# Four-layer gated mix on Trainium2: the second attention's mask as one float32r product in place of two float16 products

## The chip, the cores and the metric

The kernel runs on one core of one Trainium2 chip. The metric is the time of one execution in device microseconds (us), read as the median of several runs. Instruction durations come from one profiled execution.

## What is computed

Four layers follow one another on x, 8 sequences of 128 tokens by 128 features. Each layer adds a gated attention-like part and then a gated feed-forward part. The change touches the attention of the second of the three softmax attentions (layer index 2), which has 16 heads of depth 8, a key mask and a matrix of group probabilities:

```python
logits = jnp.einsum('bhqd,bhkd->bhqk', q, k) / jnp.sqrt(jnp.asarray(dh, q.dtype))
neg = (1.0 - mask.astype(q.dtype)) * -1000000000.0
logits = logits + neg[:, None, :, :]
attn = jax.nn.softmax(logits, axis=-1)
attn = attn * group_prob[:, None, :, :]
out = jnp.einsum('bhqk,bhkd->bhqd', attn, v)
```

So -1e9 is added to every masked score of all 16 heads, in every sequence.

## The kernel before

The program is written engine by engine: PE (matrix products), DVE, ACT, POOL (elementwise) and SP (transfers) each run a fixed order of instructions, and counters (semaphores) tie them. Nothing is reordered at run time, so an instruction that waits holds up all that stand behind it on its engine.

Attention a = 1 (the one above) goes over 8 blocks b, one for each sequence. Heads go in four sets j = 0..3 of four heads; a set fills one PSUM bank of 128 x 512. For each block there are these steps:

- **Row scores**, `att_rows` (L1204): for two sets at a time (p = 0, then p = 1), 8 small products (L1214) give the scores with queries on the partitions; then, for each of the two sets, the mask is added by products of a diagonal matrix with the mask NMA, broadcast over the four heads (all products made through the helper `products` show as L194). I call the two halves R0 and R1.
- **Maxima**: DVE reduces each set (L1235). After the fourth, five small DVE instructions of 128 x 16, here called the split (`att_max_split`: L1245, L1247, L1249, L1251, L1253), write the maximum as three float16 parts. PE turns them (`att_max_pe`, L1266), and DVE adds them to the queries (L1275).
- **Column scores**, `att_cols` (L1278), halves C0 and C1: 8 small products (L1288) give scores minus maximum with keys on the partitions, and the mask NMB is added in the same way, to banks 2 and 3.
- ACT takes the exponential of each set (L1306), **POOL multiplies it by the group probabilities** (`att_group`, L1310), and PE sums (L1323) and applies the values (L1329) in `att_pv`.
- DVE normalises (L1337, L1341), ACT and DVE split the result in high and low parts (L1348, L1356), PE applies the output weights, DVE adds to X (L1374) and starts the next layer's norm: statistics (L338, L344), POOL makes the factor (L348, L350), DVE applies it (L354), PE turns it (L405).

PE's order within block b is: C0(b); R1(b+1); `att_pv` of block b-1 for sets 2 and 3; C1(b); L1266 for b+1; output product of b-2; R0(b+2); `att_pv` of block b for sets 0 and 1; from b = 3 on the turn L405 of block b-3; then C0(b+1). C0(b+1) needs the exponentials of block b and the queries of b+1; R1(b+1) needs the first two maxima of b+1; L1266 needs the whole split; from b = 3 on L405 needs the addition to X of block b-2.

DVE's order within block b is: maxima 0 and 1 of b+1; L1356 and L413 of earlier blocks; maxima 2 and 3 of b+1; split of b+1; normalise b-1; L1275 of b+1; L354 of b-3; L1374, L338, L344 of b-2.

The mask constant is made from two float16 diagonals, DGH (-61024 on the diagonal) and DGL (-11.15625), each times 16384 (NMA, NMB) where the key is masked. They are written once by DVE in `later_dve` (L312), in front of the first softmax attention.

Of the kernel before, what the change touches and what calls it, by code (L numbers as in the profile page):

```python
# [8 lines left out]
NB, S, D = 8, 128, 128  # L9
# [19 lines left out]

B_ROW = ((0, 1), (2, 3))  # L30

MASK_UNIT = 16384.0
MASK_HI, MASK_LO = -61024.0, -11.15625
ROUND = 1.5 * 2.0 ** 23
MAX_UNITS = (16384.0, 16.0, 1.0)

# [1 line left out]
def gated_mix_program(nc, t, out):  # L38
    fp32, fp16, bf16 = mybir.dt.float32, mybir.dt.float16, mybir.dt.bfloat16
    i32, u32 = mybir.dt.int32, mybir.dt.uint32  # L40
    ALU, ACT, AX = mybir.AluOpType, mybir.ActivationFunctionType, mybir.AxisListType.X

    ctx = ExitStack()
    with ctx:
        def sb(name, shape, dt=fp32):
            return ctx.enter_context(nc.sbuf_tensor(name, shape, dt))
# [3 lines left out]
        def sem(name):  # L50
            if name not in sems:
                sems[name] = ctx.enter_context(nc.semaphore(name))
            return sems[name]

        def over(ap, n):

            p, m = ap.shape
            return ap.unsqueeze(1).to_broadcast([p, n, m])
# [17 lines left out]
        EYE, EYEH = sb("EYE", [128, 128]), sb("EYEH", [128, 128], fp16)  # L76
# [12 lines left out]
        B1 = sb("B1", [128, CH0])  # L89
        B2F, B2H, B2L = sb("B2F", [E0, D]), sb("B2H", [E0, D], fp16), sb("B2L", [E0, D], fp16)  # L90
        GPT = sb("GPT", [128, NB, S])
        NMA, NMB = sb("NMA", [128, NB, S], fp16), sb("NMB", [128, NB, S], fp16)
        DGH, DGL = sb("DGH", [128, 128], fp16), sb("DGL", [128, 128], fp16)
        IOTA = sb("IOTA", [128, 8])
        CW = sb("CW", [128, NB, 128], fp16)
        CT = sb("CT", [128, TOK], fp16)
# [31 lines left out]
        def bank(i, n=1):  # L128
            return PS[:, 512 * i:512 * (i + n)]
# [61 lines left out]
        def products(pe, dst, pairs, start=True, stop=True):  # L191

            for i, (l, r) in enumerate(pairs):
                last = pe.matmul(dst, l, r, start=start and i == 0, stop=stop and i == len(pairs) - 1)  # L194
            return last
# [116 lines left out]
        def later_dve(dve):  # L312

            dve.wait_ge(sem("ld_brow"), 16)
            dve.tensor_copy(BH[:], BF[:]).then_inc(sem("b_split"), 1)
            dve.wait_ge(sem("b_split"), 1)
            dve.tensor_tensor(BL[:], BF[:], BH[:], ALU.subtract).then_inc(sem("b_split"), 1)
            dve.wait_ge(sem("ld_bqk"), 16)
            dve.wait_ge(sem("ld_lom"), 16)
            for a in range(2):  # L320
                dve.tensor_scalar(BQK[:, a, 0, :], BQK[:, a, 0, :], DH ** -0.5, None, ALU.mult).then_inc(sem("scaled"), 1)
            dve.wait_ge(sem("scaled"), 2)
            for i in range(2):
                dve.tensor_scalar(LOB[:, :, i, :], BQK[:, :, i, :], LOM[:, i:i + 1], None, ALU.mult).then_inc(sem("lob"), 1)
            dve.tensor_scalar(DGH[:], EYE[:], MASK_HI, None, ALU.mult).then_inc(sem("eyes"), 1)
            dve.tensor_scalar(DGL[:], EYE[:], MASK_LO, None, ALU.mult).then_inc(sem("eyes"), 1)
            dve.wait_ge(sem("ld_masks"), 16)
            for i, m in enumerate((NMA, NMB)):

                dve.tensor_scalar(m[:].rearrange("p b s -> p (b s)"), MI[:, i, :], -MASK_UNIT, MASK_UNIT,  # L330
                                  ALU.mult, ALU.add).then_inc(sem("eyes"), 1)
            dve.wait_ge(sem("ld_fb1"), 16)
            dve.tensor_scalar(FB1G[:], FB1[:], G[:, 5:6], None, ALU.mult).then_inc(sem("eyes"), 1)
# [870 lines left out]
        def att_rows(pe, a, b, p):  # L1204

            n = NB * a + b
            if p == 0 and b in (0, 4):
                pe.wait_ge(sem("p_lo"), PROJ * a + (14 if b == 0 else 18))
            if 4 * n + 2 * p:
                pe.wait_ge(sem("a_max"), 4 * n + 2 * p)  # L1210
            for g in range(4):
                for j in (2 * p, 2 * p + 1):
                    r = slice(32 * j, 32 * j + 3 * DH)
                    last = pe.matmul(bank(j % 2)[:, 128 * g:128 * g + 128], QU[r, g, b, :], KU[r, g, b, :],  # L1214
                                     start=g == 0, stop=a == 0 and g == 3)
                    if a == 0 and g == 3:
                        last.then_inc(sem("a_rows"), 1)
            for j in (2 * p, 2 * p + 1):
                if a == 1:
                    products(pe, bank(j % 2), [(d[:], over(NMA[:, b, :], 4)) for d in (DGH, DGL)], start=False)\  # L1220
                        .then_inc(sem("a_rows"), 1)
                if a == 2:
                    products(pe, bank(j % 2), [(FLIP[:], biased(TBH[:, 0], j))], start=False).then_inc(sem("a_rows"), 1)

        def biased(table, j):

            return table.rearrange("p (g j s) -> p g j s", g=4, j=4)[:, :, j, :]
# [50 lines left out]
        def att_cols(pe, a, b, u, p):  # L1278

            n = NB * a + b  # L1280
            if p == 0:
                pe.wait_ge(sem("a_qx"), n + 1)
            if 4 * n + 2 * p:
                pe.wait_ge(sem("a_exp"), 4 * n + 2 * p)
            for g in range(4):
                for j in (2 * p, 2 * p + 1):
                    r = slice(32 * j, 32 * j + 32)
                    last = pe.matmul(bank(2 + j % 2)[:, 128 * g:128 * g + 128], KU[r, g, b, :], QX[r, u, g, :],  # L1288
                                     start=g == 0, stop=a == 0 and g == 3)
                    if a == 0 and g == 3:  # L1290
                        last.then_inc(sem("a_cols"), 1)
            for j in (2 * p, 2 * p + 1):
                if a == 1:
                    products(pe, bank(2 + j % 2), [(d[:], over(NMB[:, b, :], 4)) for d in (DGH, DGL)], start=False)\
                        .then_inc(sem("a_cols"), 1)
                if a == 2:
                    products(pe, bank(2 + j % 2), [(FLIP[:], biased(tb[:, 1], j)) for tb in (TBH, TBL)], start=False)\
                        .then_inc(sem("a_cols"), 1)
# [81 lines left out]
        def att_pe(pe, a):  # L1380
            k, j = NEXT[a]
            if a == 2:
                pe.wait_ge(sem("t5_split"), 12)
                pe.wait_ge(sem("ld_flip"), 16)
            att_rows(pe, a, 0, 0)
            att_rows(pe, a, 0, 1)
            att_max_pe(pe, a, 0, 0)
            att_rows(pe, a, 1, 0)
            pe.wait_ge(sem("p_lo"), PROJ * (a + 1))
            for b in range(NB):  # L1390
                u = b % 2
                att_cols(pe, a, b, u, 0)
                if b + 1 < NB:
                    att_rows(pe, a, b + 1, 1)
                if b >= 1:
                    att_pv(pe, a, b - 1, 1 - u, 2)
                    att_pv(pe, a, b - 1, 1 - u, 3)
                att_cols(pe, a, b, u, 1)
                if b + 1 < NB:
                    att_max_pe(pe, a, b + 1, 1 - u)  # L1400
                if b >= 2:
                    att_out(pe, a, b - 2, u)
                if b + 2 < NB:
                    att_rows(pe, a, b + 2, 0)
                att_pv(pe, a, b, u, 0)
                att_pv(pe, a, b, u, 1)
                if j and b >= 3:
                    turn_one_pe(pe, a, j, k, b - 3)
# [260 lines left out]
        def _(dve):  # L1669
# [10 lines left out]
            route_dve(dve, 0)  # L1680
            moe_dve(dve, 0)
            later_dve(dve)
            norm_dve(dve, 2)
            proj_dve(dve, 0, "vk")
# [161 lines left out]
```

## Time and profile before

| | us |
|---|---|
| median of 3 runs | 740.63 |
| lowest, highest | 739.57, 746.64 |
| the profiled execution's own time | 742.89 |
| its span, first to last instruction | 741.1 |
| second softmax attention, first row scores to last turn (L405) | 273.45 to 359.5 |

The page gives busy shares of the span: PE 84%, DVE 78%, ACT 48%, POOL 43%. The span is divided into 40 slices of 18.5 us; the attention in question fills slices 15 to 19. "Granted clock" is 1.00 at TensorE's 2.4 GHz level and 0.50 at its 1.2 GHz level.

How to read it: in a timeline, the time between the starts of two products is what the first one occupies of PE. Its printed duration is longer, since products are pipelined (0.38 us for a product whose successor starts 0.22 us later). A bracket such as [0.40 <-ACT ...] is the idle time of that engine ahead of the row, and what ended it.

### The profile page before, as it was taken

To read this page: it belongs to the slowest core of one execution; us is meant where nothing else is said; L and a number is where in the kernel's file an instruction comes from. 1 tells how busy PE (TensorE), PEld (TensorE's weight loads), DVE (VectorE), ACT (ScalarE), POOL (GpSimd) and SP (SyncE) were. 2 spreads that over 40 slices of the span, in tenths; PEclk is the share of its full clock that TensorE was granted. 3 is DMA by queue.
4 is the path that set the end of the run, shared out by engine and by line. 5 is a ranking of instruction groups with operands and counts; after the bars stand their busy time and mean duration, and the time that the engine had idled before them with its cause. 6 is when DMAs were issued, how large, how long until landed. Compare 5 with 4: busy or idle time off the path is not lost.

```text
span 741.1 us, 16834 instructions
## 1 busy us (share of the span) xinstructions
PE 620.3 (84%) x5152; PEld 301.1 (41%) x5152; DVE 577.3 (78%) x1174; ACT 358.4 (48%) x665; POOL 315.7 (43%) x578
## 2 busy tenths in 40 slices
PE   3774999978676577998289999999999879994996
PEld 2432433433355233555134444444444424552442
DVE  6684877777797685787769999999999785675796
ACT  4645889854453161233045455545545472341543
POOL 2486677631047202767325455444444100225241
PEclk9986999986799597999589999999999897996899
DMA  8000111105000000000011112112112000000120
GB/s 280 3 1 18 44 47 46 47 16 139 1 3 3 0 1 1 3 2 2 12 34 53 50 52 57 53 51 57 53 50 58 19 1 2 2 3 12 37 52 29
DMA packets 42346, 25.78 MB, mean 35 GB/s; under 512 B 13308, under 2 KB 41224, under 8 KB 42168
## 3 DMA queue, kind: packets, MB, share of 16 engines
q1 hardware_dynamic: 41864, 24.38, 11.6%
q8 instruction: 32, 0.52, 0.3%
q10 hardware_dynamic: 432, 0.73, 0.3%
q14 instruction: 18, 0.15, 0.1%
HBM read 24.54 MB, written 0.56 MB: 34 GB/s over the span
## 4 chain that ended last, share of the span: by engine, by line
PE 61%; DVE 22%; POOL 7%; ACT 4%; issue 4%; DMA 0%; ACTq 0%; DVEq 0%; POOLq 0%
PE PS L194 50%; DVE SHARED L1201 4%; DVE MB L1235 3%; PE PS L1214 2%; PE PS L1323 2%; DVE MF L1235 2%; PE PS L1329 1%; DVE REC L1337 1%; ACT SHARED L939 1%; PE PS L1288 1%; POOL RSTD L350 1%; DVE XN L354 1%; DVE STAT L338 1%; POOL RSTD L376 1%; PE PS L1266 1%
## 5 line engine op out<-in xcount | busy, mean ns | idle before, releaser
L950 ACT ACTIVATE SHARED<-SHARED 128x512 f16<-128x512 f32 x180 | 113.4, 630 | 120.9 <-DVE SHARED L962 114.4
L968 DVE TENSOR_TENSOR SHARED<-SHARED 128x512 f16<-128x512 f32 x180 | 141.5, 793 | 28.1 <-ACT SHARED L950 27.5
L194 PE MATMUL PS<-XH,UH 128*128 128x512 f16 x296 | 114.3, 386 | 2.4 <-ACT CT L769 2.2
L194 PE MATMUL PS<-XL,UH 128*128 128x512 f16 x296 | 114.2, 386 | 0.0
L194 PE MATMUL PS<-XH,UL 128*128 128x512 f16 x296 | 114.2, 386 | 0.0
L194 PE MATMUL PS<-SHARED,DNH 128*128 128x512 f16 x360 | 107.1, 379 | 6.4 <-DVE SHARED L968 6.2
L1306 ACT ACTIVATE SHARED<-PS 128x512 f32<-128x512 f32 x96 | 52.4, 595 | 99.5 <-PE PS L194 75.2
L959 DVE TENSOR_TENSOR SHARED<-SHARED,PS 128x512 f32<-128x512 f32 x116 | 78.6, 678 | 11.4 <-PE PS L194 11.4
L881 POOL CAST DNH<-DF 128x128 f16<-128x128 f32 x90 | 30.4, 338 | 132.0 <-PE PS L194 132.0
L962 DVE TENSOR_TENSOR SHARED<-SHARED,PS 128x512 f32<-128x512 f32 x116 | 79.7, 687 | 4.0
L871 POOL TENSOR_TENSOR UL<-UF,UH 128x256 f16<-128x256 f32 (+1 forms) x90 | 71.6, 796 | 7.2
L194 PE MATMUL PS<-SHARED,DNL 128*128 128x512 f16 x180 | 68.2, 379 | 0.0
L934 ACT ACTIVATE SHARED<-PS 128x512 f32<-128x512 f32 x116 | 62.3, 584 | 4.7 <-PE PS L194 4.6
L1310 POOL TENSOR_TENSOR SHARED<-SHARED,GPT 128x512 f32<-128x512 f32 x32 | 40.0, 1270 | 42.8 <-ACT SHARED L1306 42.8
L869 POOL CAST UH<-UF 128x256 f16<-128x256 f32 (+1 forms) x90 | 42.0, 467 | 33.7 <-PE PS L194 30.3
L1235 DVE TENSOR_REDUCE MB<-PS 128x4 f16<-128x512 f32 x64 | 41.2, 688 | 19.0 <-PE PS L194 13.9
L194 PEld LDWEIGHTS PS<-SHARED,DNH 128*128 128x128 f16 x360 | 33.3, 97 | 53.1 <-issue 21.3
L939 ACT ACTIVATE SHARED<-PS,B 128x512 f32<-128x512 f32 x64 | 43.4, 678 | 10.9 <-PE PS L194 8.4
L194 PEld LDWEIGHTS PS<-XH,UH 128*128 128x128 f16 x296 | 29.2, 99 | 45.8 <-issue 11.5
L883 POOL TENSOR_TENSOR DNL<-DF,DNH 128x128 f16<-128x128 f32 x90 | 41.5, 461 | 7.2
L194 PE MATMUL PS<-CT,SEL 128*128 128x512 f16 x116 | 44.5, 383 | 0.0
L194 PEld LDWEIGHTS PS<-XH,UL 128*128 128x128 f16 x296 | 29.4, 99 | 36.2 <-issue 2.2
(272 smaller groups left out, 1108.1 us busy)
## 6 DMA issues: line engine op xcount, KB each, us to landing
UF<-in_up SPq DMA_DIRECT2D x58, 128.0 KB, 2.0
DF<-in_down SPq DMA_DIRECT2D x90, 64.0 KB, 1.8
UF<-in_up SPq DMA_DIRECT2D x32, 64.0 KB, 1.8
SHARED<-t_values_dram SPq DMA_DIRECT2D x2, 1024.0 KB, 11.2
SEL<-in_sel SPq DMA_DIRECT2D x58, 32.0 KB, 1.8
SHARED<-in_masks SPq DMA_DIRECT2D x1, 1024.0 KB, 6.7
WF<-in_wsmall SPq DMA_DIRECT2D x1, 808.0 KB, 6.7
X<-in_x SPq DMA_DIRECT2D x1, 512.0 KB, 3.5
```

The lines of the kernel that those rows point to most:

```text
L194: last = pe.matmul(dst, l, r, start=start and i == 0, stop=stop and i == len(pairs) - 1)
L869: pool.tensor_copy(UH[:, u, 0:n], UF[:, u, 0:n]).then_inc(sem("e_up_ready"), 1)
L871: pool.tensor_tensor(UL[:, u, 0:n], UF[:, u, 0:n], UH[:, u, 0:n], ALU.subtract)\
L883: pool.tensor_tensor(DNL[:, u, :], DF[:, u, :], DNH[:, u, :], ALU.subtract)\
L934: act.activation(SG[:, hf, :], bank(hf), ACT.Silu).then_inc(sem("e_act"), 1)
L939: act.activation(RH[u][:, hf, :], bank(hf), ACT.Relu, bias=B1[:, bass.ds(c, 1)]).then_inc(sem("e_act"), 1)
L950: act.activation(HHI[:, u, hf, :], (HF if M["gated"] else RH[u])[:, hf, :], ACT.Copy).then_inc(sem("e_high"), 1)
L959: dve.tensor_tensor(TG[:, hf, :], SG[:, hf, :], bank(2 + hf), ALU.mult).then_inc(sem("e_gated"), 1)
L962: dve.tensor_tensor(HF[:, hf, :], TG[:, hf, :], bank(4 + hf), ALU.mult).then_inc(sem("e_hidden"), 1)
L968: dve.tensor_tensor(HLO[:, u, hf, :], src[:, hf, :], HHI[:, u, hf, :], ALU.subtract).then_inc(sem("e_low"), 1)
L1235: dve.tensor_reduce(dst, src, AX, ALU.max, negate=True).then_inc(sem("a_max"), 1)
L1306: act.activation(PF[:, j, :], bank(2 + j % 2), ACT.Exp).then_inc(sem("a_exp"), 1)
```

## The change

The two float16 diagonals become one float32r diagonal, and the masks become float32r. 10000 = 625 x 16 and -100000 = -3125 x 32 multiply to -1e9 with 10 and 12 significant bits. Each mask addition is then one product in place of two: per block 8 products where there were 16.

```diff
-MASK_UNIT = 16384.0
-MASK_HI, MASK_LO = -61024.0, -11.15625
+MASK_UNIT = 625.0 * 16.0
+MASK_DIAG = -3125.0 * 32.0
@@ tiles
-        NMA, NMB = sb("NMA", [128, NB, S], fp16), sb("NMB", [128, NB, S], fp16)
-        DGH, DGL = sb("DGH", [128, 128], fp16), sb("DGL", [128, 128], fp16)
+        NMA, NMB = sb("NMA", [128, NB, S], f32r), sb("NMB", [128, NB, S], f32r)
+        DGH = sb("DGH", [128, 128], f32r)
@@ later_dve
-            dve.tensor_scalar(DGH[:], EYE[:], MASK_HI, None, ALU.mult).then_inc(sem("eyes"), 1)
-            dve.tensor_scalar(DGL[:], EYE[:], MASK_LO, None, ALU.mult).then_inc(sem("eyes"), 1)
+            dve.tensor_scalar(DGH[:], EYE[:], MASK_DIAG, None, ALU.mult).then_inc(sem("eyes"), 1)
@@ att_rows
-                    products(pe, bank(j % 2), [(d[:], over(NMA[:, b, :], 4)) for d in (DGH, DGL)], start=False)\
+                    products(pe, bank(j % 2), [(DGH[:], over(NMA[:, b, :], 4))], start=False)\
@@ att_cols
-                    products(pe, bank(2 + j % 2), [(d[:], over(NMB[:, b, :], 4)) for d in (DGH, DGL)], start=False)\
+                    products(pe, bank(2 + j % 2), [(DGH[:], over(NMB[:, b, :], 4))], start=False)\
```

## Rows read from the trace of the kernel before

**Rows 1.** Chain that ended last, in block 2: start, us, work.
```profile
304.36 0.55 PE PS L194 x2
...
306.25 0.62 DVE MB L1245
```

**Rows 2.** Timeline of PE, block 2: start, us, instruction.
```profile
302.66 0.40 PE L1288 MATMUL PS<-QX,SHARED 32*128 32x128 f16 x8
302.99 0.39 PE L194 MATMUL PS<-NMB,DGH 128*128 128x512 f16 x1
303.22 0.38 PE L194 MATMUL PS<-NMB,DGL 128*128 128x512 f16 x1
...
306.27 0.40 PE L1288 MATMUL PS<-QX,SHARED 32*128 32x128 f16 x8
...
307.82 0.40 PE L1266 MATMUL PS<-EYEH,MB 128*128 128x128 f16 x4 [0.18 <-DVE MB L1253]
...
310.73 0.40 PE L1288 MATMUL PS<-QX,SHARED 32*128 32x128 f16 x8
```

**Rows 3.** Timelines of ACT and POOL, block 2.
```profile
303.63 1.09 ACT L1306 ACTIVATE SHARED<-PS 128x512 f32<-128x512 f32 x2 [2.16 <-PE PS L194]
...
304.31 2.49 POOL L1310 TENSOR_TENSOR SHARED<-SHARED,GPT 128x512 f32<-128x512 f32 x2 [1.68 <-ACT SHARED L1306]
307.92 2.51 POOL L1310 TENSOR_TENSOR SHARED<-SHARED,GPT 128x512 f32<-128x512 f32 x2 [1.11 <-ACT SHARED L1306]
```

**Rows 4.** Timeline of DVE, block 2: parts of the split.
```profile
306.25 0.60 DVE L1245 TENSOR_SCALAR MB<-MF 128x16 f16<-128x16 f32 x1
...
307.35 0.18 DVE L1251 SCALAR_TENSOR_TENSOR MF<-MB,MF 128x16 f32<-128x16 f16 x1
307.56 0.20 DVE L1253 CAST MB<-MF 128x16 f16<-128x16 f32 x1
```

**Rows 5.** Timelines of POOL, DVE and PE around the split of block 1.
```profile
288.12 2.48 POOL L1310 TENSOR_TENSOR SHARED<-SHARED,GPT 128x512 f32<-128x512 f32 x2 [0.40 <-ACT SHARED L1306]
...
288.26 1.15 DVE L1251 SCALAR_TENSOR_TENSOR MF<-MB,MF 128x16 f32<-128x16 f16 x1
289.45 1.21 DVE L1253 CAST MB<-MF 128x16 f16<-128x16 f32 x1
...
290.72 0.40 PE L1266 MATMUL PS<-EYEH,MB 128*128 128x128 f16 x4 [2.88 <-DVE MB L1253]
...
294.61 0.60 PE L1288 MATMUL PS<-QX,SHARED 32*128 32x128 f16 x8
```

**Rows 6.** Timelines of PE and DVE in the later blocks.
```profile
327.54 0.30 PE L405 MATMUL PS<-EYE,XN 128*128 128x128 f32 x1 [0.19 <-DVE X L1374]
327.78 0.40 PE L1288 MATMUL PS<-QX,SHARED 32*128 32x128 f16 x8
...
334.29 1.42 DVE L354 TENSOR_SCALAR XN<-X,MV,RSTD 128x128 f32<-128x128 f32 x1
...
344.92 0.40 PE L1288 MATMUL PS<-QX,SHARED 32*128 32x128 f16 x8
```

**Rows 7.** Windows: us, busy (count) of PE, PEld, DVE, ACT, POOL, granted clock.
```profile
182.70:186.00 3.30, 3.30 (x8) 1.19 (x9) 0.75 (x1) 1.30 (x2) 0.00 (x0) 0.50 0.00 0
292.00:295.00 3.00, 3.00 (x42) 1.73 (x40) 1.38 (x2) 0.00 (x0) 0.00 (x0) 0.50 0.00 0
596.30:600.00 3.70, 3.63 (x20) 1.74 (x20) 3.70 (x6) 2.88 (x5) 0.00 (x0) 1.00 0.00 0
612.20:616.00 3.80, 2.84 (x24) 1.14 (x24) 1.72 (x3) 0.00 (x0) 0.00 (x0) 0.57 0.00 0
```

**Rows 8.** Lines L1523 and L330 (ns min/median/max), and a timeline row of L384.
```profile
L1523 PE MATMUL PS<-OH,RB x2: 1031/1044/1056, 52.7 to 53.6; 32*16 32x512 f32 x2
...
179.57 1.04 PE L384 MATMUL PS<-EYE,XN 128*128 128x128 f32 x8
...
L330 DVE TENSOR_SCALAR NMA<-SHARED x1: 684/684/684, 167.6 to 167.6; 128x1024 f16<-128x1024 int32 x1
```

More of the change, by code:

```diff
@@ L40, in gated_mix_program @@
     i32, u32 = mybir.dt.int32, mybir.dt.uint32
+    f32r = mybir.dt.float32r
     ALU, ACT, AX = mybir.AluOpType, mybir.ActivationFunctionType, mybir.AxisListType.X
```

## The prediction

> **What bounds the kernel now.** I read the page first (PE 84% busy, DVE 78%), then the chain of waits in the second softmax attention, then timelines of each engine for one block, since only there one sees who is late. In block 2 the chain runs through PE's mask products into DVE's maxima and the split [rows 1]: PE looks like the bound, 8.07 us from one C0 to the next (302.66 to 310.73) [rows 2], of which 16 mask products at some 0.22 us (302.99 to 303.22) are 3.5 us. But look further. POOL works in pairs of multiplies of 2.49 us, and the second pair starts 1.12 us after the first has ended (304.31 + 2.49 = 306.80; 307.92) [rows 3]. L1245 of the split, 0.20 us when free, starts at 306.25 and takes until 306.85, just after POOL's pair ends; the rest of the split then fits in the gap, its last instruction starting 0.36 us before POOL's second pair [rows 3, 4]. And around the split of block 1, where POOL's pair came 0.14 us ahead of L1251, L1251 took 1.15 us (until 289.41, POOL's first multiply ending near 289.36) and L1253 1.21 us (until 290.66, POOL's second ending at 290.60), against 0.18 and 0.20 [rows 4, 5]. So each of these DVE instructions waits for the end of the POOL multiply that is running. L354, 0.34 us when free, takes 1.42 us in the later blocks for the same reason [rows 6]. The kernel runs well as long as the split slips through POOL's gap.
>
> **The mask products, size.** A float16 product of 512 columns occupies 0.215 to 0.22 us. No row shows float32r. Bounds: a float32 product of 512 columns is two instructions 0.9 us apart at the low clock, so 0.9 us in all at the high one [rows 8]; that is the upper end. The middle: 8 float32 transposes of 128 columns take 1.04 us, 0.11 us each from start to start, so a single pass over 512 columns of float32 could be 0.43 us [rows 8]. The lower end is float16's 0.215 us. 
>
> **What that does in block 2 if each product is 0.215 us.** Four products go between C0 and C1: 4 x 0.2175 = 0.87 us. C0 to C1 is now 306.27 - 302.66 = 3.61 us, then 2.74 us. POOL's first pair starts 1.65 us after C0 now; one product fewer ahead of the first exponential makes it 1.43 us. It ends at C0 + 3.92. The second pair can start at 2.74 + 1.43 = C0 + 4.17: a gap of 0.25 us in place of 1.12 us. The maxima come 0.65 us earlier (three products), but that is worth nothing: L1245 waits for the end of the pair, and after it L1251 starts 0.55 us and L1253 0.76 us past the pair's end (307.35 and 307.56 against 306.80) [rows 4]. Now both find POOL busy, as in block 1. L1253 ends with POOL's second pair, at 4.17 + 2.49 + 0.05 = C0 + 6.71, and L1266 starts at C0 + 6.76 instead of 5.16 (307.82 - 302.66). Behind L1266 on PE stand the output product, R0 and `att_pv`, then the next C0: 2.91 us now, 2.48 us with two products fewer. A block takes 6.76 + 2.48 = 9.24 us, 1.17 us more than 8.07.
>
> **Later blocks.** They take 8.57 us (two from 327.78 to 344.92). Add the turn of 0.24 us (327.54 to 327.78) to the sum above [rows 6]: 9.48 us. The wait of PE for L1374 goes, since L354 now starts after POOL's pair. The last of the intervals has no R0 and is led by DVE: some 9.1 us. From C0 of block 1 to C0 of block 7 it is now 344.92 - 294.61 = 50.31 us [rows 5, 6]; then 2 x 9.24 + 3 x 9.48 + 9.1 = 56.0 us: **+5.7 us**.
>
> **Ends.** Blocks 0 and 1 already have the hold and a low clock; their mask products cost about 0.43 us each in the low stretch, and four of them go ahead of the second pair: -1.7 us, of which I keep -1.5 us (bounds -3 and 0). After the last C0 POOL's four multiplies run without a gap and set the end; only one product goes ahead of them: -0.2 us.
>
> **Clock.** In a block of 9.24 us, C1's last result is there 2.74 + 0.33 + 0.22 + 0.38 = 3.7 us after C0, and L1266 starts at 6.76: PE stands idle for 3.1 us. The kernel has six idle stretches of PE of 2.1 to 2.9 us that begin at the high clock, and after each of them the granted clock falls to the low level (0.50 to 0.58) for 3 us or more; after one of 1.9 us it doesn't (596.30 to 600.00 at 1.00) [rows 7] (the group has the stretch behind the first and the last of the six, and the one behind block 1's idle 2.88 us). In block 1 the stretch from L1266 to C0 took 294.61 - 290.72 = 3.89 us against 2.91, and the 8 products behind it 0.60 against 0.40 [rows 2, 5]: at least 1.2 us. Three us at half speed are 1.5 us lost if PE leads all the while. I take 1.4 us for each of six blocks: **+8.4 us**.
>
> **Conversions.** DVE writes one diagonal less (-0.1 us) and two masks of 4 bytes in place of 2, 0.68 us each now [rows 8], at most twice that. PE works on values and keys meanwhile, and DVE's own next long piece of work there waits for ACT. I price this at 0; without that cover up to +1.2 us.
>
> **Sum.** 742.89 + 5.7 - 1.5 - 0.2 + 8.4 = 755.3 us for the profiled execution, which stands 2.3 us above the median. Against the median: 740.63 + 12.4 = **753 us**.
>
> The Trainium skill (SBUF — State Buffer, Who interferes with whom) says that DVE and GpSimd share a pair of ports, that whichever issues first holds it for its whole instruction, and that the other blocks. It names casts and instructions with two SBUF inputs, which L1253 and L1251 are. The rows above agree (1.15 and 1.21 us against 0.18 and 0.20), and the sum rests on them.
>
> **Rivals.**
> - The holds come but the clock stays high: 740.63 + 5.7 - 1.7 = 745 us. For it: a boundary of the low stretch may fall kindly, and a 1.9 us gap did no harm. Against: six of six. 0.18.
> - The other side: the split still gets through POOL's gap, so blocks get shorter. Then the split ends 0.22 us earlier (C0 + 4.94), and a block is 4.94 + 2.48 = 7.4 us early on, and some 8.0 us later, where POOL's second pair ends 0.6 us earlier and L354 with it: about -0.6 us each, -3.6 us, and -1.7 us at the ends: 735 us. It decides where the gap is over 0.76 us: C0 to C1 must be 3.25 us, so four products must cost 0.51 us more than I think, 0.34 us each; or DVE's small instructions must win against POOL where they lost in block 1. 0.16, since later blocks have R1 held by the maxima, which widens the gap.
> - The change saves no PE time, at 0.43 us for each product: distances stay as they are, 741 us. For it: the transposes. 0.14.
> - A product costs float32's 0.9 us: 8 x 0.45 = 3.6 us more for each block, less about 1 us of slack: +20 us, 761 us. 0.05.
> - My forecast: 0.47.
>
> **Range and chances.** The forecast's own range is 747 to 763 (clock cost of 0.5 to 2.7 us a block). 8 in 10 reach from the upper half of the second rival to there: 736 to 762. A measurement of this kernel tells about 1% from no change, 7.4 us. Faster by that: only a strong form of the second rival, below 733.2: 0.11. Same: the first and third rivals and most of the second, 0.18 + 0.14 + 0.05 = 0.37 (what the first spills over to the slow side, the low end of my forecast gives back). Slower: the forecast and float32's price, 0.47 + 0.05 = 0.52.
>
> **What would show it.** Mask products 64 in place of 128, at 0.21 to 0.22 us from start to start (else the size is wrong). L1251 and L1253 at 1.2 us in most blocks, and L1266 waiting for L1253 by 2 us and more (else the hold is wrong). POOL's two pairs 0.2 to 0.4 us apart. From C0 to C0 over 9 us. Stretches of low granted clock in blocks 2 to 6. If the split runs in 1 us and blocks take 8 us or less, I am wrong on the sign.

## The result: 757 us, 1.6% slower, and the profile after

The changed kernel takes 757.26 us (750.1 to 761.2, 4 runs) against 740.48 us on the same chip: ratio 1.0164, 95% interval 1.0101 to 1.0227. The ratio is estimated over runs in the fast state; the two medians as they stand are 2.3% apart. So the change makes the kernel slower beyond the noise, and whether by more than 2% is open. The profiled execution takes 761.20 us, its span is 759.4 us.

The rows of the changed kernel. First PE in block 3, and the turn from block 4's C0 on (start, us, instruction, idle time ahead of it). The helper `products` is line 195 now.

```profile
320.78 0.40 PE L1288 MATMUL PS<-QX,SHARED 32*128 32x128 f16 x8
321.11 0.73 PE L195 MATMUL PS<-NMB,DGH 128*128 128x512 f32 x2
321.77 0.40 PE L1214 MATMUL PS<-SHARED 24*128 24x128 f16 x8
...
323.78 0.40 PE L1288 MATMUL PS<-QX,SHARED 32*128 32x128 f16 x8
324.10 0.73 PE L195 MATMUL PS<-NMB,DGH 128*128 128x512 f32 x2
327.91 0.61 PE L1266 MATMUL PS<-EYEH,MB 128*128 128x128 f16 x4 [3.08 <-DVE MB L1253]
...
332.94 0.60 PE L1288 MATMUL PS<-QX,SHARED 32*128 32x128 f16 x8
333.48 1.22 PE L195 MATMUL PS<-NMB,DGH 128*128 128x512 f32 x2
...
338.19 0.40 PE L1288 MATMUL PS<-QX,SHARED 32*128 32x128 f16 x8
338.51 0.73 PE L195 MATMUL PS<-NMB,DGH 128*128 128x512 f32 x2
339.09 0.40 PE L1266 MATMUL PS<-EYEH,MB 128*128 128x128 f16 x4
```

One set's mask addition is one product now, so a half (C0, C1, R0 or R1) has two. The two occupy PE for 321.77 - 321.11 = 0.66 us, and between C0 and C1 lie four mask products fewer than before. So C0 to C1 is 3.00 us (323.78 - 320.78) against 3.61 us in [rows 2]. But L1266 starts 7.13 us after C0 instead of 5.16, after 3.08 us of idle time.

POOL and DVE in the same block, beside [rows 3] and [rows 4]:

```profile
322.32 2.51 POOL L1310 TENSOR_TENSOR SHARED<-SHARED,GPT 128x512 f32<-128x512 f32 x2
325.31 2.48 POOL L1310 TENSOR_TENSOR SHARED<-SHARED,GPT 128x512 f32<-128x512 f32 x2 [0.48 <-ACT SHARED L1306]
...
323.96 0.93 DVE L1245 TENSOR_SCALAR MB<-MF 128x16 f16<-128x16 f32 x1
324.92 0.18 DVE L1247 SCALAR_TENSOR_TENSOR MF<-MB,MF 128x16 f32<-128x16 f16 x1
325.13 0.20 DVE L1249 TENSOR_SCALAR MB<-MF 128x16 f16<-128x16 f32 x1
325.37 1.23 DVE L1251 SCALAR_TENSOR_TENSOR MF<-MB,MF 128x16 f32<-128x16 f16 x1
326.64 1.21 DVE L1253 CAST MB<-MF 128x16 f16<-128x16 f32 x1
```

POOL's gap is 0.48 us, not 1.12. L1247 and L1249 run in it; L1251 comes 0.06 us behind the start of POOL's second pair and takes 1.23 us, L1253 1.21 us. I call an instruction of DVE held when it ends only with the POOL multiply that is running, as these two do. In blocks 1 and 5 only L1253 is held in this way (1.22 and 1.20 us). In block 3 both are on the chain that ended last (start, us, work):

```profile
322.64 1.30 DVE MF L1235 x2
...
323.96 0.94 DVE MB L1245
...
325.37 1.25 DVE MF L1251
...
326.64 1.23 DVE MB L1253
...
327.91 0.61 PE PS L1266 x4
```

The windows of blocks 1 to 5 (us; busy and count of PE, PEld, DVE, ACT, POOL; granted clock, DMA share, GB/s):

```profile
304.00:311.00 7.00, 5.15 (x91) 3.27 (x94) 5.69 (x11) 2.28 (x5) 5.01 (x4) 0.99 0.00 1
311.00:317.50 6.50, 6.50 (x76) 3.79 (x68) 3.58 (x11) 1.09 (x2) 2.50 (x2) 0.50 0.01 3
317.50:325.00 7.50, 7.33 (x119) 4.56 (x115) 5.99 (x13) 2.73 (x6) 5.84 (x6) 0.99 0.01 3
...
328.50:337.50 9.00, 9.00 (x93) 5.48 (x94) 4.99 (x14) 1.68 (x4) 3.31 (x4) 0.50 0.01 2
338.00:347.00 9.00, 8.08 (x132) 4.87 (x124) 8.14 (x20) 3.66 (x8) 6.12 (x7) 0.99 0.01 2
```

The granted clock goes high, low, high, low, high, and what PE waits for goes with it. In a block that runs at the high level the split is held and PE sits idle: in block 1 for 1.85 us (ahead of 309.02), in block 3 for 3.08 us (ahead of 327.91), in block 5 for 1.85 us again. The clock falls behind that. In the block at the low level C0 to C1 takes 5.25 us (332.94 to 338.19), POOL's two pairs lie 2.24 us apart, nothing holds the split, and L1266 doesn't wait (339.09). Then the clock rises and the hold is back.

**Stages of the attention**, from the timelines (us). "Start" is from the first row scores to C0(1), then the six intervals C0(1) to C0(7), and the "tail" from there to the last L405. `before2` and `again2` are the two kernels profiled once more.

| | start | six intervals | tail | attention | ahead of it | behind it |
|---|---|---|---|---|---|---|
| before | 21.15 | 50.31 | 14.12 | 85.58 | 273.46 | 382.06 |
| before2 | 19.62 | 50.06 | 14.10 | 83.78 | 279.48 | 379.64 |
| after | 18.70 | 59.37 | 13.70 | 91.77 | 283.73 | 383.90 |
| again | 18.66 | 59.35 | 13.69 | 91.70 | 275.74 | 378.56 |
| again2 | 18.68 | 59.39 | 13.70 | 91.77 | 280.47 | 383.96 |

So the attention takes 6.2 us more than before (8.0 against `before2`, where block 1's hold is absent). The six intervals take 9.3 us more against `before2`, the start 0.9 us less and the tail 0.4 us less. In the profile of after another 10.3 us lie ahead of the attention and 1.8 us behind it, where the change touches little.

### The profile page after: what moved, and what is told of

Same layout as the page of the kernel before. It is cut to its first block, busy times and chain, and to the rows that moved or that the text cites. A ratio compares the mean times of both kernels' runs of the same rounds, so it can differ in the third digit from the quotient of the medians.

```text
span 759.4 us, 16705 instructions
## 1 busy us (share of the span) xinstructions
PE 638.9 (84%) x5088; PEld 311.9 (41%) x5088; DVE 577.9 (76%) x1173; ACT 359.1 (47%) x665; POOL 314.8 (41%) x578
## 4 chain that ended last, share of the span: by engine, by line
PE 65%; DVE 20%; POOL 5%; ACT 5%; issue 4%; DMA 1%; ACTq 0%; DVEq 0%; POOLq 0%
PE PS L195 50%; DVE SHARED L1201 3%; DVE MB L1235 3%; PE PS L1323 2%; PE PS L1214 2%; PE PS L1329 2%; PE PS L1288 1%; ACT SHARED L939 1%; DVE MF L1235 1%; PE PS L584 1%; DVE STAT L338 1%; DVE REC L1337 1%; PE PS L1266 1%; POOL RSTD L350 1%; POOL RSTD L376 1%
```

## The experiments

In the experiments' kernels lines shift by one to four (POOL's multiply is L1312 in `after_poolwait`, for instance). Medians come from interleaved runs with the kernel before on the same chip, and a ratio is always to the kernel before. "Attention" is the stage of the table above.

**The same kernel again, twice.**

> The changed kernel once more, in five rounds. Of the 18.3 us by which its profiled span exceeds the one before, 10.3 us lie ahead of the second attention's first row scores (283.73 against 273.45), in code that the change does not touch, where the granted clock was 0.50 from 20 to 60 us in place of 1.00 and 0.74. Chance theory: that part varies from execution to execution in either kernel, and the change itself costs only what the attention shows, +6 to +8 us; then the runs fall in two groups some 8 to 10 us apart, near 748 to 753 and 758 to 762, and the kernel before has such outliers too. Layout theory: the change shifts that part always; then all runs lie near 757 to 762. Expected: the first, median 750 to 757.

> The changed kernel a third time, for the profile alone. The attention took 91.8 and 91.7 us in two profiles, with the same alternation of long and short blocks. Chance theory: the same again within 1 us, and the parts ahead and behind differ from run to run. If the attention varies by several us, my comparison of stages is too narrow.

Measured: `again` 753.14 us (747.78 to 761.58, 6 runs), ratio 1.0164 (1.0105 to 1.0222). `again2` 757.94 us, one run. The attention takes 91.70 and 91.77 us, with the same intervals block for block. Inside the attention the slowdown is fixed; what varies lies outside.

**The kernel before, once more.**

> The kernel before once more, for the profile alone: how far do the parts ahead of and behind the second attention vary by themselves? Chance theory: they differ from the first profile's 273.5 and 382.1 us by 2 us or more in some of these repeats, while the attention stays within 1 us of 85.6.

Measured: 744.72 us in one run, attention 83.78 us, 1.8 us from the first profile's and not within the 1 us that I had expected; the parts ahead and behind differ by 6.0 and 2.4 us. Its block 1 has no hold (L1253 201/202/203 ns, least, median, most), so the hold in [rows 5] is not there in each execution, and 1.5 of the 1.8 us lie in the start (19.62 against 21.15 us), where that split runs.

**Take the collision away.** POOL's second pair waits until the split is done:

```diff
 def att_group(pool, b, j):
     pool.wait_ge(sem("a_exp"), 4 * (NB + b) + j + 1)
+    if j == 2 and b + 1 < NB:
+        pool.wait_ge(sem("a_msplit"), 5 * (b + 1) + 5)
```

> The changed kernel, and POOL waits before the third multiply of a block until DVE has finished the next block's split (no work removed). Hold theory: L1251 and L1253 run at 0.2 us in every block, PE never waits over 1 us for L1253 in blocks 2 to 6, the granted clock stays at 1.00 there, and C0 to C0 takes 7.4 us in the early blocks and about 8.1 us in the later ones, where L354 still waits for POOL's pair: 8 to 12 us below the changed kernel, about 735 to 742. Size theory (the 4-byte products are what makes it slower, the hold is a by-product): no faster than the changed kernel, 750 or more.

Measured: 742.49 us (737.81 to 750.98, 10 runs), ratio 0.9983 (0.994 to 1.0027). Attention 81.44 us, 10.3 less than after, six intervals 49.10 us. Lines of the split over all eight blocks, POOL and PE in block 2:

```profile
L1251 DVE SCALAR_TENSOR_TENSOR MF<-MB,MF x8: 178/179/180, 283.6 to 341.3; 128x16 f32<-128x16 f16 x8
L1253 DVE CAST MB<-MF x8: 202/204/205, 283.8 to 341.5; 128x16 f16<-128x16 f32 x8
...
305.44 2.51 POOL L1312 TENSOR_TENSOR SHARED<-SHARED,GPT 128x512 f32<-128x512 f32 x2 [1.27 <-ACT SHARED L1306]
309.05 2.50 POOL L1312 TENSOR_TENSOR SHARED<-SHARED,GPT 128x512 f32<-128x512 f32 x2 [1.10 <-DVE MB L1253]
...
308.96 0.40 PE L1266 MATMUL PS<-EYEH,MB 128*128 128x128 f16 x4 [1.01 <-DVE MB L1253]
```

The products are the changed kernel's; only POOL's start has moved, from a gap of 0.48 us (block 3 of after) to one of 1.10 us. L1251 and L1253 are at 0.18 and 0.20 us in each block, as expected; blocks take 7.7 to 7.9 us early and 8.38 us later, somewhat more than the 7.4 and 8.1 us forecast, and the median stands just above the forecast's 742. The hold goes and the slowdown goes with it, in the attention and in the whole kernel. POOL's pair starts later than its data are there, and PE still waits less, since the split no longer takes turns with POOL.

**The product's size apart from its type.** The kernel before with its high diagonal alone, one float16 product for each set. C0 to C1 is then what I forecast for float32r:

```diff
-[(d[:], over(NMB[:, b, :], 4)) for d in (DGH, DGL)]
+[(d[:], over(NMB[:, b, :], 4)) for d in (DGH,)]
```

> The kernel before with float16 diagonals, but with DGL and its products left out: one float16 product for each mask addition, so that the constant is -0.99982e9 in place of -1e9. This is the change with products of 0.215 us, as I had priced them, where float32r products measured about 0.34 us. Hold theory: C0 to C1 falls from 3.61 to 2.74 us, POOL's pairs come 0.25 us apart, L1251 and L1253 are both held in most blocks, PE idles 3 us and the low clock follows: slower than before by 8 to 16 us, 748 to 757. Size theory: half the mask products gone at no cost, so faster than before by 5 us or more, below 736.

> The same float16 kernel with DGL and its products left out (the constant is -0.99982e9), and POOL waits before the third multiply of a block for the next split. Hold theory: the split runs in 1 us everywhere, blocks take 7.2 us early and 8.0 us later, about 5 to 9 us below the kernel before: 732 to 736. Size theory: the wait only delays POOL, equal to or slower than the same kernel without it.

Measured: `high_only` 756.57 us (755.72 to 758.4, 4 runs), ratio 1.0192 (1.0131 to 1.0253), attention 98.98 us. A kernel with half the mask work is 1.9% slower than before. Block 2 shows it, in PE, POOL and DVE:

```profile
306.04 0.39 PE L1287 MATMUL PS<-QX,SHARED 32*128 32x128 f16 x8
306.37 0.61 PE L194 MATMUL PS<-NMB,DGH 128*128 128x512 f16 x2
...
308.78 0.40 PE L1287 MATMUL PS<-QX,SHARED 32*128 32x128 f16 x8
...
313.02 0.61 PE L1265 MATMUL PS<-EYEH,MB 128*128 128x128 f16 x4 [3.30 <-DVE MB L1252]
...
310.21 2.48 POOL L1309 TENSOR_TENSOR SHARED<-SHARED,GPT 128x512 f32<-128x512 f32 x2 [0.23 <-ACT SHARED L1305]
...
310.28 1.25 DVE L1248 TENSOR_SCALAR MB<-MF 128x16 f16<-128x16 f32 x1
311.57 1.16 DVE L1250 SCALAR_TENSOR_TENSOR MF<-MB,MF 128x16 f32<-128x16 f16 x1
```

C0 to C1 is 2.74 us (308.78 - 306.04) and the gap 0.23 us, both as I had worked out (2.74 and 0.25). The split is held in every block, and PE waits 1.9 to 3.3 us for it in each of blocks 0 to 6. Here the clock cost and the hold do add up: the low stretch behind 313.02 is over by 319.5, ahead of the next C1, so that the next split meets POOL's pair again. `high_only_poolwait` takes 738.37 us (734.99 to 748.35, 10 runs), ratio 0.9946 (0.9902 to 0.9989), attention 79.10 us: 19.9 us less than `high_only`, with L1252 at 202 ns. That is above the 732 to 736 us forecast (blocks of 7.44 and 8.26 us for 7.2 and 8.0). It is the fastest kernel here that computes the whole attention, half a per cent below the kernel before; its added constant is -16384 x 61024 = -0.99982e9 instead of -1e9.

**Take POOL's multiply away, without and with the change.** Both kernels leave the group probabilities out of the result, so they serve for timing alone.

```diff
-            if a == 1:
-                pe.wait_ge(sem("a_group"), 4 * b + j + 1)
-            src = PG if a == 1 else PF
+            src = PF
@@ POOL's program
-                    for j in range(4):
-                        att_group(pool, b, j)
```

> The kernel before with POOL's multiply by the group probabilities left out in the second attention; the values are applied to the exponentials. Nothing can hold DVE's split or L354 there. Both theories: somewhat faster than before, by L354's 1.1 us in four blocks, L1245's 0.3 us and block 1's hold: 5 to 8 us. It is the base for the next run.

> The changed kernel with the same multiply left out. Hold theory: without POOL's multiply the change brings what PE saves. Two products take 0.66 us up to the next work in place of 0.97 us for four, so four such places give 1.24 us a block where PE leads: 7 to 9 us faster than before_nogroup, and no low clock in blocks 2 to 6. Size theory (the 4-byte products are slow in themselves, or bring the clock down): as slow as before_nogroup or slower.

Measured: 741.72 us (736.69 to 745.39, 10 runs), ratio 0.9977 (0.9937 to 1.0016), attention 78.17 us, without the change; 729.86 us (727.29 to 730.64, 4 runs), ratio 0.9829 (0.9767 to 0.9891), attention 72.57 us, with it. The first is a miss for the kernel as a whole: the attention is 5.6 to 7.4 us shorter than before, as forecast, and the median is not. With the change, the split is never held and C0 to C1 takes 2.99 us. One against the other the change gains 5.6 us in the attention and 11.9 us between medians. So the saving on PE is real, and it is the meeting with POOL's multiply that turns it into a loss. The attention's gain is a little under what I had expected for it; that of the medians is above it, and the difference lies outside the attention.

**The wait alone, without the change.** The same two lines of `att_group` in the kernel before.

> The kernel before, and POOL waits before the third multiply of a block for the next split. Hold theory: only block 1's split was held, so that this is worth at most its 2 us plus the low clock behind it, 1 to 4 us; blocks 2 to 6 as before, 8.07 and 8.57 us. Size theory, by which the wait helps in any kernel: 8 us or more, as in the changed kernel.

Measured: 741.79 us (740.12 to 750.68, 10 runs), ratio 1.0013 (0.9966 to 1.006), attention 83.82 us, as in `before2`. The wait changes nothing beyond the noise where the split slips through anyway. It gains in the two kernels that lost by the hold.

**Keep PE busy behind C1, with the hold in place.** 18 products of 128 x 256 into an unused half bank ahead of L1266:

```diff
+    if a == 1 and b + 1 < NB:
+        for _ in range(18):
+            pe.matmul(bank(6)[:, 256:512], EYEH[:], CHI[:, 0:2, :], start=True, stop=True, skip_group_check=True)
```

> The changed kernel with 18 float16 products of 256 columns added on PE ahead of each turn of the maxima L1266 (about 2.0 us, into an unused half of bank 6, nothing reads them), so that PE isn't idle while DVE's split is held. It parts the hold from the clock. My forecast's sum added 8.4 us for the clock to 5.7 us for the hold; if they add, the attention from first row scores to last L405 falls from 91.7 to 84 to 86 us. Exchange theory: a block at the low clock is slow, but in it POOL's pairs are so far apart that the split isn't held, so that hold and low clock take turns; with the clock kept high, every block is held, each takes 9.7 to 10 us and the attention stays at 90 to 93 us.

Measured: 750.80 us (748.71 to 752.9, 2 runs), ratio 1.0108 (1.002 to 1.0196), attention 92.18 us. In block 5:

```profile
341.51 2.14 PE L1401 MATMUL PS<-CHI,EYEH 128*128 128x256 f16 x18
344.75 0.40 PE L1266 MATMUL PS<-EYEH,MB 128*128 128x128 f16 x4 [1.10 <-DVE MB L1253]
...
342.15 2.48 POOL L1310 TENSOR_TENSOR SHARED<-SHARED,GPT 128x512 f32<-128x512 f32 x2 [0.47 <-ACT SHARED L1306]
...
342.23 1.22 DVE L1251 SCALAR_TENSOR_TENSOR MF<-MB,MF 128x16 f32<-128x16 f16 x1
343.49 1.21 DVE L1253 CAST MB<-MF 128x16 f16<-128x16 f32 x1
```

PE's idle time falls to 1.1 us, the granted clock stays high from block 1 on (mean over the attention 0.91 against 0.74 in after), and the attention is no faster. C0 to C1 is 2.99 us from block 1 on and the hold comes back in each block, each 9.5 to 10.0 us long. That settles how the two costs go together in the changed kernel: they take turns. The six intervals in pairs take 19.2, 20.0 and 19.5 us here, with a hold in each block and the clock high, and 18.4, 21.2 and 19.8 us in after, with one block of each pair held and its neighbour slow; without either, 15.6 to 16.8 us (`after_poolwait`). Block 3 of after does pay for both (12.16 us), and its neighbour gets it back by having no hold (9.02 us). Adding a clock loss to every block was wrong here.

**Push POOL's second pair further**, behind L354 of the same block too, to free L354 as well (from b = 3 on):

```diff
     if j == 2 and b + 1 < NB:
         pool.wait_ge(sem("a_msplit"), 5 * (b + 1) + 5)
+        if b >= 3:
+            pool.wait_ge(sem("ln_xn"), NB * 5 + b - 2)
```

> The changed kernel with POOL waiting before the third multiply for the next split and, from block 3 on, for L354 too, so that neither is held. Hold theory: the later blocks lose L354's 1.1 us hold as well and take about 7.6 us in place of 8.38; attention 78 to 79 us after 81.4; whole kernel 737 to 741. Against it: POOL's second pair then ends later, and if att_pv of sets 2 and 3 waits for it, nothing is won.

> The same in the kernel with one float16 product for each mask addition (DGL left out, constant -0.99982e9): later blocks about 7.4 us in place of 8.25, attention 75 to 76 us, whole kernel 733 to 737. Against it: as above.

Measured: 743.23 us (741.42 to 750.93, 10 runs), ratio 1.0008 (0.9963 to 1.0053), attention 83.40 us, 2.0 us more than `after_poolwait`; with the high diagonal alone 742.88 us (737.85 to 747.16, 10 runs), ratio 0.9969 (0.9932 to 1.0005), attention 82.25 us, 3.2 us more than `high_only_poolwait`. Both are misses. DVE and POOL in a later block of `after_poolwait2` (L1360 is L1356 before):

```profile
318.63 0.93 DVE L1360 TENSOR_TENSOR ATL<-AT,ATH 128x128 f16<-128x128 f32 x1
...
321.65 1.17 DVE L1247 SCALAR_TENSOR_TENSOR MF<-MB,MF 128x16 f32<-128x16 f16 x1
...
324.90 0.34 DVE L354 TENSOR_SCALAR XN<-X,MV,RSTD 128x128 f32<-128x128 f32 x1
...
320.28 2.50 POOL L1314 TENSOR_TENSOR SHARED<-SHARED,GPT 128x512 f32<-128x512 f32 x2
325.41 1.27 POOL L1314 TENSOR_TENSOR SHARED<-SHARED,GPT 128x512 f32<-128x512 f32 x1 [2.63 <-DVE XN L354]
```

L354 is free (0.34 us), but the second pair now reaches into the next block, where it meets L1360 (0.93 us instead of 0.28), and POOL's next first pair, pushed on by it, meets L1247 (1.17 instead of 0.18). PE waits 1.59 us for the split there. The hold has moved one place on, so the later blocks gain nothing: the six intervals take 49.37 us against 49.10. Most of the 2.0 us lies in the tail (15.36 against 13.67 us), where the last held-back pair of POOL starts 1.4 us later than in `after_poolwait` (343.28 against 341.88) and the four last multiplies and all the rest stand behind it.

## Why the prediction was right on the sum, and what in it was not

The forecast was 753 us, slower, range 736 to 762; the medians are 757.26 and 753.14 us. Point by point:

- **The product's size: mis-sized.** I took 0.215 us and bounded it by 0.215, 0.43 and 0.9. Between the two products of a half lie 0.34 us (0.22 us in `high_only`), and the second occupies 0.32 us (0.31). So it is about half as long again, but only between two of its kind. A float16 load of the diagonal takes 95 to 100 ns, the float32r one 186 ns and up (ns least/median/most; the median holds low-clock blocks):

```profile
L195 PEld LDWEIGHTS PS<-NMA,DGH x32: 186/288/338, 284.1 to 355.2; 128*128 128x128 f32 x32
...
L330 DVE TENSOR_SCALAR NMA<-SHARED x1: 689/689/689, 175.8 to 175.8; 128x1024 fp32r<-128x1024 int32 x1
```

  Between C0 and C1 the change saves 0.61 us (3.61 to 3.00) where I had 0.87, and `high_only` saves just 0.87. The second row is the mask's conversion: 689 ns against 684 in [rows 8], priced at 0, rightly.
- **POOL's gap: right in kind, 0.48 us for 0.25.** I had put the point from which the split escapes at a gap of 0.76 us, "0.34 us each" for four products. The product came out at 0.34 us, and the split doesn't escape: four of them cost 3.00 - 2.74 = 0.26 us more than float16's, not 0.51, since each half pays the longer step only once, and C0 to C1 is 3.00 us, short of the 3.25 us that decided. The distance was the right measure, the price of one instruction wasn't.
- **The hold: right.** In block 3 L1251 takes 1.23 us and L1253 1.21 us beside POOL's multiply, and neither is held in `after_poolwait` and `after_nogroup`. L1266 waits 3.08 us in block 3 (forecast 3.1).
- **In every block: wrong for this product size.** It comes in blocks 1, 3 and 5, not in 2, 4 and 6, and of the two instructions that I had held in each block, L1251 is held in block 3 alone. With the clock kept high (`after_fill`) both are held in blocks 1 to 6: the alternation comes from the clock.
- **Clock: it falls behind a hold, as forecast, but doesn't add to one in each block.** I had the six intervals at +5.7 for holds and +8.4 us for the clock, 14.1 in all; after has 59.37 - 50.31 = +9.1 us. Holds alone, at the high clock, cost 58.64 - 50.31 = +8.3 us (`after_fill`, 298.44 to 357.08), so the term for holds was too small and that for the clock, +0.7 us on top of it, far too large. With 0.215-us products (`high_only`) it is 65.26 - 50.31 = +15.0 us: for its own product size the sum was nearly right, start -1.2 and tail -0.4 included (+13.4 us in the attention, forecast +12.4). The rule that I put beside it, six of six, was misread from the trace of before: ahead of 268.17 PE idles for 2.14 us from the high clock and the clock stays at 1.00 (rows below). The rival in which the clock stays high had more for it than I allowed.
- **Start and tail:** -2.5 us for -1.5, -0.4 us for -0.2. Against `before2`, whose block 1 has no hold, the start is only 0.9 us shorter, so part of the -2.5 us is a hold that comes and goes in the kernel before.
- **Two slips of arithmetic:** a clock cost of 2.7 us a block gives 740.63 + 5.7 - 1.7 + 16.2 = 761 us as the forecast's upper end, not 763; and what the chance of "same" takes from the second rival is 0.05 of 0.16, not most of it, although that rival's own 735 us lies within "same". Neither changes the forecast.
- **The total.** The attention gives +6.2 to +8.0 us, half to two thirds of the forecast's +12.4. The medians give +16.8 us in the first set of runs and +10.3 us in the second; over all 11 runs the changed kernel's median is 753.5 us. So 753 us came so near since a term that was too large met a part outside the attention that I had not foreseen. That closeness is partly luck; the sign and the mechanism are not.

**What stays open** is that part outside, some 2 to 11 us (10.3 - 8.0 to 16.8 - 6.2). In the profile of after the stretch from 20 to 40 us ran at the low clock and in that of before at the high one, with the same work in the program (same columns as the windows above; the first row is of after, the second of before):

```profile
20.00:40.00 20.00, 19.26 (x150) 8.69 (x148) 8.88 (x24) 10.91 (x40) 6.91 (x12) 0.50 0.01 2
```

```profile
20.00:40.00 20.00, 16.10 (x208) 8.37 (x206) 13.14 (x40) 13.57 (x52) 10.22 (x20) 1.00 0.01 2
```

The runs show scatter of this kind, by the clock, in either kernel. Executions of the kernel before with a mean granted clock of 0.908 take 739.5 to 740.0 us, those with 0.884 take 748.5 to 748.9 us. The same idle stretch of PE is followed by the low clock in one execution and not in the next. One of 2.14 us stands just ahead of this attention in before, and one of 2.13 us at the same instruction in `before2` (first the row of PE and the window behind it in before, then the window in `before2`):

```profile
268.17 0.39 PE L194 MATMUL PS<-XH,WRH 128*128 128x512 f16 x1 [2.14 <-DVE XL L396]
...
268.17:272.17 4.00, 4.00 (x19) 1.84 (x20) 2.33 (x4) 3.14 (x5) 0.00 (x0) 1.00 0.00 0
```

```profile
272.54:276.54 4.00, 4.00 (x11) 1.49 (x12) 1.16 (x2) 1.74 (x3) 0.00 (x0) 0.58 0.00 0
```

Of 14 profiles the clock stays high behind this stretch in three (before, `high_only_poolwait`, `after_nogroup`), and these three have the shortest time ahead of the attention, 273.5 to 274.4 us; the others have up to 283.7 us, in after and in `before_nogroup` alike. The time behind the attention runs from 378.5 to 384.0 us. Over the seven profiles of kernels with float16 masks and the seven with float32r masks the means differ by 1.1 us ahead (276.9, 278.0) and by less than 0.1 us behind (380.8, 380.9), so no effect of the mask's type outside the attention is shown. Why the clock falls behind a stretch in one execution and not in another stays open, and with it how much of a few us between two medians is the kernels' own. The two kernels without POOL's multiply show the same: 5.6 us apart in the attention, 11.9 us between medians.

The Trainium skill (SBUF — State Buffer, Who interferes with whom) has DVE and GpSimd share a pair of ports that one of them holds for a whole instruction while the other blocks. The runs agree: 1.21 us for a cast that takes 0.20 us alone, and 0.20 us in all eight blocks once POOL's multiply is kept away from it or taken out.

## What to carry to other kernels

Before shortening the work between two long POOL instructions, look at which small DVE instructions run in the gap between them: here saving 0.6 us of PE work between C0 and C1 closed a gap of 1.12 us to 0.48 us and put L1266 2 us later. Then give POOL's start an explicit wait for those DVE instructions; it cost nothing measurable where it wasn't needed (ratio 1.0013, 0.9966 to 1.006) and gave back 10 us of attention time where it was. And check the moved instruction against the next neighbours on DVE: one place too far and the hold comes back there.

## What the runs showed of the hardware that I had not expected

- Two float32r products of 512 columns follow each other by 0.34 us at the high clock, between float16's 0.22 us and the 0.9 us worked out for float32 from [rows 8], and loading 128 x 128 float32r weights takes 186 ns against 97. Whether the load or the stream sets the 0.34 us was not tried.
- The length of an idle stretch alone doesn't tell whether the clock falls. Behind 1.85 us of idle time (ahead of 309.02 and of 348.04 in after) it fell; behind 1.88 us in `high_only` (ahead of 323.86), 1.9 us in before [rows 7] and 2.14 us in before (ahead of 268.17) it stayed high. The low stretch lasted from 311 to about 317.5 behind the first, and until about 338 behind the 3.08 us ahead of 327.91.
- A low clock can hide the conflict of DVE and POOL: blocks 2, 4 and 6, which began at 0.50, had no held split and took 9.01 to 9.02 us in after; the held ones at the high level took 9.5 to 10.0 us in `after_fill`.
